# Four-layer stage of a language-model tower: 64-row and 64-column halves of the TensorE array in place of block-diagonal 128x128 operands

## The reference

```python
def _linear_attn(x, Wq, Wk, Wv, Wo, bo):          # 8 heads of 8 features
    q = softmax(split(x @ Wq) * scale, axis=-1)   # over the 8 features of a head
    k = softmax(split(x @ Wk) * scale, axis=-2)   # over the 256 tokens
    v = split(x @ Wv)
    context = einsum('bhnd,bhne->bhde', k, v)
    out = einsum('bhnd,bhde->bhne', q, context)
    return merge(out) @ Wo + bo

for i in range(4):
    x = x + _linear_attn(layernorm(x, ln1[i]), Wq[i], Wk[i], Wv[i], Wo[i], bo[i])
    x = x + gelu(layernorm(x, ln2[i]) @ W1[i] + b1[i]) @ W2[i] + b2[i]
```

## Time and profile before

| | us |
|---|---|
| median of 3 runs | 677.21 |
| the 3 runs | 674.14, 677.21, 679.40 |
| the profiled execution, its own time | 670.27 |
| its span, first to last instruction | 668.50 |
| TensorE busy | 559.0 |
| VectorE busy | 425.2 |
| ScalarE busy | 402.9 |

### The profile page before, as it was taken

How to read it: one execution, slowest core, us unless ns; L and a number is a source line. 1 busy time by engine, 2 the same in 40 slices (tenths; PEclk the granted TensorE clock), 3 DMA queues, 4 the chain that set the end, 5 groups by cost and what they waited for, 6 DMA issues and landing times.

```text
span 668.5 us, 8276 instructions
## 1 busy us (share of the span) xinstructions
PE 559.0 (84%) x2840; PEld 292.8 (44%) x2862; DVE 425.2 (64%) x1105; ACT 402.9 (60%) x673; POOL 25.0 (4%) x36
## 2 busy tenths in 40 slices
PE   0688993599899999749989988988873998999995
PEld 0345883343333333536656655655632333333331
DVE  6789577735433635498998998998775344333333
ACT  0468211467676677326888788778742665766663
POOL 8060000000000000000000000000000000000000
PEclk9988795699999999779999999999977899999998
DMA  7902000000000000300000000000000000001001
GB/s 225 201 1 48 1 1 0 1 0 1 0 1 0 1 1 0 94 1 1 1 0 1 1 2 0 1 1 1 2 0 1 0 1 0 1 1 31 1 0 31
DMA packets 16344, 11.03 MB, mean 16 GB/s; under 512 B 10065, under 2 KB 15217, under 8 KB 16241
## 3 DMA queue, kind: packets, MB, share of 16 engines
q1 hardware_dynamic: 14000, 9.93, 5.7%
q10 hardware_dynamic: 2304, 0.58, 0.5%
HBM read 9.47 MB, written 1.05 MB: 16 GB/s over the span
## 4 chain that ended last, share of the span: by engine, by line
PE 67%; DVE 13%; ACT 11%; issue 3%; DMA 3%; SPq 1%; DVEq 0%; ACTq 0%
PE bank L1520 19%; PE bank L1536 18%; ACT Hd L712 6%; PE bank L1666 4%; PE bank L1601 3%; ACT L712 3%; PE bank L1657 3%; DMA w1m<-in_w1e 3%; PE bank L1646 2%; PE bank L1608 2%; PE bank L1525 2%; PE bank L1616 2%; PE bank L1627 2%; PE bank L1327 2%; DVE Ph L951 1%
## 5 line engine op out<-in xcount | busy, mean ns | idle before, releaser
L652 ACT ACTIVATE Hd<-bank,b1all 128x512 f32<-128x512 f32 x256 | 155.1, 690 | 73.0 <-PE bank L1520 73.0
L1536 PE MATMUL bank<-Hd,w2m 128*64 128x512 f32 x512 | 123.1, 604 | 5.0 <-issue 5.0
L1059 DVE SCALAR_TENSOR_TENSOR Tmp<-bank,b2col,Wb 128x512 f32<-128x512 f32 x56 | 42.0, 751 | 129.3 <-PE bank L1536 129.2
L1520 PE MATMUL bank<-Ph,w1m 64*128 64x512 f32 x256 | 67.6, 632 | 3.6 <-ACT Hd L652 2.1
L1520 PE MATMUL bank<-XT,w1m 64*128 64x512 f32 x256 | 67.3, 636 | 3.9 <-ACT CT L636 1.7
L1536 PEld LDWEIGHTS bank<-Hd,w2m 128*64 128x64 f32 x512 | 31.5, 136 | 52.4 <-issue 51.5
L1608 PE MATMUL bank<-bd,XT 128*128 128x128 f32 x256 | 36.7, 290 | 15.1 <-ACT Hd L712 15.0
L1608 PEld LDWEIGHTS bank<-bd,XT 128*128 128x128 f32 x256 | 32.8, 200 | 27.6 <-ACT Hd L712 26.6
L1520 PEld LDWEIGHTS bank<-XT,w1m 64*128 64x128 f32 x256 | 23.9, 192 | 40.1 <-ACT Hd L652 21.6
L1520 PEld LDWEIGHTS bank<-Ph,w1m 64*128 64x128 f32 x256 | 24.1, 190 | 38.6 <-ACT Hd L652 20.6
L1063 DVE TENSOR_TENSOR Rest<-Rest,Tmp 128x512 f32<-128x512 f32 x56 | 38.7, 692 | 1.9
(11 more groups left out here) (220 smaller groups left out, 903.8 us busy)
## 6 DMA issues: line engine op xcount, KB each, us to landing
Ph<-in_x SPq DMA_DIRECT2D x4, 512.0 KB, 8.6
Ph<-in_itok SPq DMA_DIRECT2D x4, 384.0 KB, 9.2
w1m<-in_w1e SPq DMA_DIRECT2D x1, 1028.0 KB, 17.4
w2m<-in_w2e SPq DMA_DIRECT2D x2, 512.0 KB, 12.6
w1m<-in_w1e SPq DMA_DIRECT2D x1, 1024.0 KB, 5.5
out<-Hs SPq DMA_DIRECT2D x16, 64.0 KB, 1.7
Hd<-in_w1all SPq DMA_DIRECT2D x1, 512.0 KB, 13.7
bd<-in_l_attn SPq DMA_DIRECT2D x8, 64.0 KB, 4.1
```

The source lines that it names most:

```text
L652: ac.activation(Hd[:, st.ring, k // 2, k % 2, :], bank[k][:, :], func, bias=b1all[:, m, st.e, k // 2:k // 2 + 1]).then_inc(up_read, 1)
L1059: ve.scalar_tensor_tensor(dst, bank[4 + st.ring][:, :], b2, Wb[:, st.ring, :], ALU.add, ALU.mult).then_inc(down_read, 1)
L1520: te.matmul(bank[k][:, :], w1m[hs, st.e, k // 2 * P:(k // 2 + 1) * P], operand[hs, gslice(st.g)], start=True, stop=True).then_inc(up_made, 1)
L1536: ins = te.matmul(bank[4 + st.ring][h * D:(h + 1) * D, :], w2m[:, st.e, hc * D:(hc + 1) * D], Hd[:, st.ring, hc, h, :], start=(hc == 0), s ...
```

## The change

The block-diagonal operands go. `w4` holds the four weights of a layer side by side, on partitions 0 to 63 and again on 64 to 127. Each product is issued per half: keys and mix in a 64x64 corner of the array, queries and values together as 64 rows by 128 columns with 128 moving columns (64 of q and 64 of v), the attention output as 64 rows by 128 columns with 64 moving columns, and the context as 128 rows by 64 columns. The four values projections that stood behind the feed-forward are gone as a step. Queries and values now fill two banks, the attention output two banks, and the bank table is new; keys now stand ahead of the mix. VectorE's mix step moves from the end of a beat to behind the next beat's keys maximum, the attention addition moves ahead, the queries' shift behind it, and the keys' reciprocal into the next gap of the softmax. ScalarE's copy of the values now waits for the queries' shift, since both read the same banks.

```diff
@@ -138,9 +138,10 @@
 JOBS = LAYERS * G
-BEAT = (("xa", 0, 5, 1), ("xf", 2, 0, 1), ("yt", 3, 2, 1), ("m", 1, 7, 1), ("k", 0, 4, 1), ("qt", 1, 0, 1),
-        ("q", 0, 3, 1), ("o", 1, 0, 1), ("fup", 2, 1, 1), ("fup", 2, 7, 2), ("fup", 2, 6, 3), ("fup", 2, 2, 4),
-        ("v", 0, 1, 1), ("kt", 0, 7, 1), ("fdown", 2, 3, 1), ("ctx", 0, 1, 1))
+BEAT = (("xa", 0, 5, 1), ("xf", 2, 0, 1), ("yt", 3, 1, 1), ("k", 0, 5, 1), ("m", 1, 6, 1), ("qt", 1, 4, 1),
+        ("qv", 0, 0, 1), ("qv", 0, 1, 2), ("o", 1, 2, 1), ("o", 1, 3, 2),
+        ("fup", 2, 7, 1), ("fup", 2, 4, 2), ("fup", 2, 6, 3), ("fup", 2, 3, 4),
+        ("kt", 0, 6, 1), ("fdown", 2, 4, 1), ("ctx", 0, 7, 1))
@@ -419,12 +428,9 @@
-            sp.wait_ge(l1_zeros, 1)
-            for layer in range(LAYERS):
-                for h in range(2):
-                    hs = slice(h * D, (h + 1) * D)
-                    sp.dma_start(bd1[hs, layer, :, hs],
-                                 a["l1_attn"][layer].rearrange("d (w n) -> d w n", w=4)).then_inc(l1w_in, 16)
+            for h in range(2):
+                sp.dma_start(w4[h * D:(h + 1) * D, :, :],
+                             a["l1_attn"].rearrange("l d c -> d l c")).then_inc(l1w_in, 16)
@@ -482,8 +488,6 @@
...
-            gp.memset(boB[:, :, :], 0.0)
-            gp.memset(bd1[:, :, :, :], 0.0).then_inc(l1_zeros, 1)
@@ -688,6 +688,11 @@
                               bias=lvecs[:, job.layer, n + 1:n + 2]).then_inc(l1_read[what], 1)
+            def values_out(job):
+                act.wait_ge(shifted, job.done)
+                ac.copy(Vt[:, job.g, :].rearrange("p (j h d) -> p j h d", j=4, h=2), qv_part(1)).then_inc(l1_read["qv"], 2)
@@ -1186,14 +1193,22 @@
                 for jb in range(2):
-                    ins = ve.scalar_tensor_tensor(Mm[:, job.ring, jb, :], l1_bank("m")[:, jb * P:(jb + 1) * P],
+                    ins = ve.scalar_tensor_tensor(Mm[:, job.ring, jb, :], l1_bank("m")[:, jb * D:(jb + 1) * D],
                                                   ksm[:, job.g, 3, jb:jb + 1], boB[:, job.layer, :], ALU.mult, ALU.add)
                 ins.then_inc(l1_read["m"], 1)
-            def add_out(what, job):
-                l1_full(dve, what, job)
-                ve.tensor_tensor(gsl(Xs, job.g), gsl(Xs, job.g), l1_bank(what)[:, :], ALU.add).then_inc(l1_read[what], 1)
+            def feed_in(job):
+                l1_full(dve, "yt", job)
+                ve.tensor_tensor(gsl(Xs, job.g), gsl(Xs, job.g), l1_bank("yt")[:, :], ALU.add).then_inc(l1_read["yt"], 1)
+            def attn_in(job):
+                b = [b for what, _, b, k in BEAT if what == "o" and k == 1][0]
+                l1_full(dve, "o", job)
+                x = gsl(Xs, job.g).rearrange("p (j h e) -> p h j e", j=4, h=2)
+                ve.tensor_tensor(x, x, banks[:, b:b + 2, 0:S].rearrange("p h (j e) -> p h j e", j=4),
+                                 ALU.add).then_inc(l1_read["o"], 2)
@@ -1240,20 +1255,21 @@
                     old = None
                 if now:
                     keys_max(now)
+                if attn:
+                    mix_out(attn)
                 if old:
                     measure("yt", old, 0, old.ring)
                 if now:
                     queries_max(now)
+                if attn:
+                    attn_in(attn)
                 if old:
                     centre(old, 0, old.ring, old.done)
+                if attn:
+                    measure("o", attn, 1, attn.ring)
                 if now:
                     queries_shift(now)
                 if attn:
-                    add_out("o", attn)
-                if now:
-                    keys_sum(now)
-                if attn:
-                    measure("o", attn, 1, attn.ring)
                     roots(attn, old)
                     centre(attn, 1, attn.ring, attn.done)
                 if old:
@@ -1268,15 +1284,16 @@
                     queries_sum(now)
                     context_out(now)
                     queries_inverse(now)
+                    keys_sum(now)
                     queries_norm(now)
                 if feed:
-                    add_out("yt", feed)
+                    feed_in(feed)
                     if feed.last:
                         finished(feed.g)
-                if now:
-                    mix_out(now)
-            dve.wait_ge(bo_ready, 2)
+            step(ve.tensor_tensor(mask[:, :], headmask[:, 0:D], headmask[:, D:P], ALU.add))
+            step.settle()
+            dve.wait_ge(bo_ready, 1)
             beat(0)
             layernorm(4, 1, Hs, Xs)
             first_norms(1)
@@ -1601,31 +1618,40 @@
                 ins.then_inc(l1_made[what], 1)
-            def project(t, what, job, w):
-                dst = l1_free(t, what)
+            def queries_values(t, job):
+                for h in range(2):
+                    l1_free(t, "qv", h + 1)
+                w = w4[:, job.layer, :].rearrange("p (w n) -> p w n", w=4)
                 for j in range(4):
-                    ins = te.matmul(dst[:, j * P:(j + 1) * P], XT[:, col(job.g, j)], bd1[:, job.layer, w, :],
-                                    start=True, stop=True)
-                ins.then_inc(l1_made[what], 1)
+                    for h in range(2):
+                        hs = slice(h * D, (h + 1) * D)
+                        ins = te.matmul(l1_bank("qv", h + 1)[:, j * P:(j + 1) * P], XT[hs, col(job.g, j)],
+                                        w[hs, 0:3:2, :], start=True, stop=True)
+                ins.then_inc(l1_made["qv"], 2)
             def keys(t, job):
                 l1_taken(pe, "xa", job)
                 dst = l1_free(t, "k")
-                te.matmul(dst[:, :], bd1[:, job.layer, 1, :], gsl(XT, job.g), start=True,
-                          stop=True).then_inc(l1_made["k"], 1)
+                for h in range(2):
+                    hs = slice(h * D, (h + 1) * D)
+                    ins = te.matmul(dst[hs, :], w4[hs, job.layer, D:2 * D], XT[hs, gslice(job.g)], start=True, stop=True)
+                ins.then_inc(l1_made["k"], 1)
             def context(t, job):
                 l1_taken(pe, "kt", job)
-                l1_taken(pe, "v", job)
+                l1_taken(pe, "qv", job)
                 dst = l1_free(t, "ctx")
                 for jb in range(2):
                     for jj in range(2):
-                        c = slice((2 * jb + jj) * P, (2 * jb + jj + 1) * P)
-                        ins = te.matmul(dst[:, jb * P:(jb + 1) * P], Vt[:, job.g, c], Kt[:, job.ring, c],
-                                        start=(jj == 0), stop=(jj == 1))
+                        j = 2 * jb + jj
+                        for h in range(2):
+                            ins = te.matmul(dst[h * D:(h + 1) * D, jb * D:(jb + 1) * D],
+                                            Vt[:, job.g, (2 * j + h) * D:(2 * j + h + 1) * D],
+                                            Kt[:, job.ring, (2 * j + h) * D:(2 * j + h + 1) * D],
+                                            start=(jj == 0), stop=(jj == 1))
@@ -1633,19 +1659,25 @@
                 for jb in range(2):
-                    ins = te.matmul(dst[:, jb * P:(jb + 1) * P], Cm[:, job.ring, jb, :], bd1[:, job.layer, 3, :],
-                                    start=True, stop=True)
+                    for h in range(2):
+                        hs = slice(h * D, (h + 1) * D)
+                        ins = te.matmul(dst[hs, jb * D:(jb + 1) * D], Cm[hs, job.ring, jb, :],
+                                        w4[hs, job.layer, 3 * D:4 * D], start=True, stop=True)
                 ins.then_inc(l1_made["m"], 1)
             def attend(t, job):
                 l1_taken(pe, "m", job)
                 l1_taken(pe, "qt", job)
-                dst = l1_free(t, "o")
+                for h in range(2):
+                    l1_free(t, "o", h + 1)
                 for j in range(4):
-                    ins = te.matmul(dst[:, j * P:(j + 1) * P], Qf[:, job.ring, j * P:(j + 1) * P],
-                                    Mm[:, job.ring, j // 2, :], start=True, stop=True)
-                ins.then_inc(l1_made["o"], 1)
+                    for h in range(2):
+                        hs = slice(h * D, (h + 1) * D)
+                        ins = te.matmul(l1_bank("o", h + 1)[:, j * D:(j + 1) * D],
+                                        Qf[hs, job.ring, j * P:(j + 1) * P], Mm[hs, job.ring, j // 2, :],
+                                        start=True, stop=True)
+                ins.then_inc(l1_made["o"], 2)
@@ -1678,21 +1710,19 @@
                 if old:
                     l1_taken(pe, "fdown", old)
                     turn(t, "yt", Yt[:, old.ring, :])
-                if last:
-                    mix(t, last)
                 if now:
                     keys(t, now)
                 if last:
+                    mix(t, last)
                     pe.wait_ge(qn_ready, last.done)
                     turn(t, "qt", Qe[:, last.g, :])
                 if now:
```

(3 more changed lines are left out.)

48 lines of the change are left out of this document (26 added, 22 removed).

## The result

| | us |
|---|---|
| before, median of 14 runs | 674.46 (671.87 to 679.40) |
| changed, median of 14 runs | 679.20 (676.84 to 685.60) |
| ratio of the runs, 95% interval | 1.0088 (1.0062 to 1.0113) |
| profiled execution before, its span | 670.27, 668.5 |
| profiled execution changed, its span | 679.3, 677.4 |

The change costs less than 1%, and its interval lies clear of no change: a small loss. The forecast for the median was 685.1, its range 671 to 697. The profiled execution of the kernel before is faster than every one of its 14 runs (lowest 671.87), that of the changed kernel is like its median; so the 8.9 us between the two spans are more than the change.

The account below looks back on a forecast made before the run. The stage was taken as bound by a loop through several engines, none full. Shorter beats -2.5, clock falls +9.4 and fill +1 gave +7.9 us on a 677.2 median: 685.1, range 671 to 697.

Parts of the forecast that it names:

- The beat: Four-layer stage, first Gelu to next first Gelu: 12.84 us instead of 13.03, a gain of 0.19 in a beat.
- TensorE's and VectorE's path together: Within a beat, both reach attention output together, at 9.4 and 9.45; VectorE's keys' maximum follows at 8.06, then the mix.
- Values, 0: In the beat, 0.9 us of TensorE values work goes, none of it in the chain: gain 0.
- The gap: TensorE idle before the turned keys, about 2.6 us instead of 1.25; 1.45 us per clock fall, 6.5 of 13 beats: +9.4.
- Fill +1: Pipeline fill: first job's attention output waits for VectorE's long layer norm and runs at low clock: +1 us (0 to 2).
- The drain: Last beats of the stage, as the pipeline empties: the forecast's sum has no separate term for a change there.
- The sum: Whole kernel: -2.5 + 9.4 + 1 = +7.9 us, on a median of 677.2 giving 685.1.
- its own case: Stage: low clock in some beats, 4 to 10 of 13; 681 to 691 us, chance 0.48.
- (1): Rival, stage: the gap stays under what drops the clock, so the clock holds: 675.7 us, chance 0.22.
- (2): Rival, stage: low clock in every beat, +17.4 us: 694.6, chance 0.09.
- (3: 0.84): Rival: 64 moving columns halve attention output to 0.45 us, beat about 12.4, clock held: 670 us, chance 0.09.
- rival 4: Array corners do not overlap: keys alone at 1.71 us give 685.6, all three kinds at double length 708; chance 0.08.

Follow-up runs that it names:

- The kernel with the mix first: The changed kernel with only the mix moved back ahead of the keys and to the end of VectorE's beat: 680.27 us, ratio to before 1.0086.
- the fillers: Four kernels: the changed kernel plus unread products ahead of the turned keys; ratios to before 0.9969 (3 x 384 columns), 0.9970 (1 x 384), 1.0086 (16 half-array), 1.0076 (4 x 16).

## Why the prediction was right, step by step

- **The beat, forecast 12.84: 12.83.** Its parts, from start to start in the timeline above: keys start at 6.72 (371.55 less 364.83; forecast 6.7) and take 0.88 (0.86); mix 0.36 (0.27); turned queries 0.58 (0.54 with passage); queries with values 1.00 (1.04 with passage); attention's output 0.84 (0.89). So it starts at 9.54, where it did before (9.53), and not at 9.4; most of the difference is the mix. From there it is 0.84 and 2.45 us (2.50) to the next Gelu, 0.1 less than forecast. The sum is right because two errors of 0.1 us cancel: the gain is attention's output without its passage, not an earlier start of it.
- **TensorE's and VectorE's path together.** Not quite: VectorE has the mix done at 374.07 in that beat (two operations in 0.48; forecast 0.40), TensorE begins attention's output at 374.37. TensorE's queue bounds. The kernel with the mix first agrees: a mix that leaves that queue gives 0.17 us, and then its turned queries wait for VectorE's norm (done at 398.33, turned from 398.69).
- **Values, 0.** Right: no wait of theirs shows in the steady beats.
- **The gap, forecast 2.6 and low clock: 2.29 and low clock.** The sign and the price were right: 1.36 us a fall (1.45). The number, seven falls in thirteen beats (6.5), was luck: the forecast says itself that no row gave it, and took the middle between never and every beat. The gap is 0.3 us shorter than forecast, mostly since feed-forward up is recorded to 12.53 in the beat, and not 12.3. The mechanism was half right. I read the length of a gap against others; the fillers show that a gap of 1.36 us falls often or hardly by what stands beside it. And the scale of gaps came from one execution: the 1.68 us that it calls survived falls in seven of fourteen traces. The kernel before was kept up by its values, eight instructions with 128 moving columns in the place where the change has none: without them, and with the turned keys a Gelu later, it has five falls; with them back in that place the changed kernel has none.
- **Fill +1: -0.3 in this trace.** First turned input to first Gelu took 33.3 us (278.79 to 312.12) against 33.6 (275.30 to 308.90). But the four kernels with fillers, the same code up to there, took 34.5 to 34.6, with about 23 us of low clock in it where the changed kernel had 13.7 and before 16.9. So the term may well be near the +1 of the forecast; how much of it is the code and how much the clock is open.
- **The drain, forecast 0: -1.8.** From the end of the 13 beats to the last beat's first Gelu it took 21.4 us against 23.2; the kernel before has two falls there, the changed one has one. Which beat of the drain falls differs from kernel to kernel.
- **The sum.** Stage 7.3 - 0.3 - 1.8 = +5.2 us, and the ratio of the medians is worth 0.0088 x 674.5 = +5.9. The forecast had +7.9. Of the distance between 685.1 and 679.2, 2.7 us are the base: 14 runs put before at 674.46 where three had given 677.21. By both, 679.2 lies under the 681 to 691 that the forecast gave to its own case, within the wider range.
- **Rivals.** The clock did not hold (1), was not low in each beat (2), 64 moving columns did not halve attention's output (3: 0.84), and corners overlap (4: keys 0.88). Two slips of the working change nothing: the times of rival 4 leave out the +1 of the fill, and the 8.06 of VectorE's path is 8.08 by its own terms. The rule of the Trainium skill that was weighed (TensorEngine Tiling (Array Packing), Tiling Modes, Key Properties: a change of shape drains the array) stands as it did: the passages cost 0.1 to 0.2 us each, and no run shows one of the 0.3 us that the forecast also priced. The one on gaps (TensorE: Matmul & The Clock Gate, Why this matters for your kernels) would have held the clock at 2.29 us; the trace shows seven falls.

## What to carry to other kernels

Work taken off TensorE beside the critical path isn't free to take: count what it leaves for the clock. Where the granted clock drops, look at the kinds of instruction around the gap as well as its length, and not at the busy share. Judge it by more than one execution, since the same gap falls in one and holds in another. A product with many moving columns on the full array there, needed or even not, may be worth more than its time. Put the halved products where they shorten the chain, and keep the large ones for the waits.

## What the runs showed of the hardware

- TensorE at the same busy time (11.35 us in 12.83) and with the same gap (1.36 us) was granted 1.00 in all but one of thirteen beats with two instructions of 384 columns in the gap, and fell in six with sixteen half-array instructions of 64 moving columns. It fell in seven with eight full-array instructions of 16 moving columns, though busier (11.50 us) and with less gap (1.20).
- A gap of 1.68 us with the same instructions around it ended in a fall in seven traces of fourteen.
- Sixteen half-array fp32 instructions in alternation took 0.94 us with 64 moving columns and 1.00 with 128, from start to start: halving the moving columns of this product saved 0.06 us. Attention's output, sixteen of 64 too, took 0.84 us in the changed kernel.
- With the low clock in it, feed-forward down took 2.96 to 3.57 us instead of 1.94, and the beat of the changed kernel 1.17 to 1.42 us more.
